# A fused cross-attention, block and router loop on one Trainium2 core: PSUM banks by stage, three choice batches, spread first weights, and block one-hots multiplied on GpSimd

## The chip, the cores and the metric

The kernel runs on one core of one Trainium2 chip. The metric is the device time of one execution in microseconds, the median over runs. The engines are named as in the profile: PE (TensorE, with PEld for its weight loads), DVE (VectorE), ACT (ScalarE), POOL (GpSimd) and SP (SyncE, which here only issues DMAs). They run their own instruction streams and meet at semaphores.

## The reference

Shapes: x is 8 sequences of 512 tokens, 512 wide; the context is 8 sequences of 77 rows. Cut to what matters:

```
x = x + cross_attention(layernorm(x), ctx)     # 16 heads of 32, softmax over 77 keys, wo, bo
h  = attention block on groups of 8 tokens      # (512 positions are the batch): LN1, qkv (4 kv heads), causal
h1 = x + proj(h)
z2 = LN2(h1);  logits = z2 @ router_weight      # 8 experts
top 2 of 8 by softmax, renormalised             # share = p1 / (p1 + p2), which needs only exp(l2 - l1)
order = stable sort of (token, choice) by expert; first `cap` rows of each expert are kept
out = h1 + scatter_add(share * gelu(xt @ w1[e]) @ w2[e])
```

## The kernel before, in words

The 4096 tokens are 32 tiles of 128. One Python loop of 52 steps (`STEPS`) writes, for every engine, what it does in step i; it is a software pipeline, in which a tile is in another stage in each step. Tile t = i − 1 is transposed (`xT`, kind `xt`), i − 2 gets its scores (and q, for two tiles at once, in even steps), i − 4 has its probabilities transposed (`pT`, four jobs of kind `pt`) and multiplied with the values (`pv`), i − 5 goes through `wo`. From step 13 the same loop also carries block tiles f, with lags from `FF` = 14: the first layer norm (statistics `mvf`, normalised tile z, kept in `ctx_then_block`) at lag FF − 1, its transposes and qkv, scores, projection, second layer norm, router logits, and at lag FF + 5 the softmax over the two best experts. So steps 3 to 13 are cross attention only, 14 to 18 fill the block's pipeline, 19 to 33 carry both, and from 36 only the block is left. The loop is followed by the choice of experts, the search for each row's slot, one-hot matrices from which PE makes the table of rows (`one_hots`), and then the experts.

What the prediction's steps touch:

- PSUM has eight banks. `psum_plan` hands them out in the order of `psum_jobs`, in turn within each half; a score job `s` takes banks 0 to 3 together. `bank_free` makes PE wait until the old user of a bank is read out.
- First layer norm of f: DVE takes the statistics (L668, L669); POOL adds and takes a power −0.5 (L508, L509, giving `rff` for z and the semaphore `rstd_f`), and then another pair with another constant (L437, L438, giving `rf` for the residual); DVE makes z (L907). After this POOL multiplies the probabilities by the softmax's reciprocals (L448).
- Router softmax of f: DVE takes the eight largest (L865) and the `gap` of the first two (L867); ACT takes `ex` = exp(gap) (L620); POOL makes the shares in five operations (L494 to L501), which stand on POOL ahead of L508.
- DVE turns q and k of the block in L879 and L883; L883 waits for `v_kept`, a copy on ACT (L615).
- Choice: `choose(a, b)` on DVE makes the 0/1 matrix `both` of tiles a to b − 1 in 10 operations (L692 to L699), at the end of a step; `count_places` on PE counts with three matmuls per tile (L934 to L938), one step later. `CHOICES` says in which step which tiles go.
- The first expert's weights come in eight pieces of 128 x 1024, one in each of the steps 39 to 46: SP loads one, ACT rounds the high part, POOL subtracts for the low part (L1155), behind everything else of its step.
- `one_hots`: eight batches of eight tiles. ACT makes the row one-hots of six tiles (`BY_ACT`; L652, L657), DVE those of the other two (L748), the block one-hots `is_blk` (L744) and their product with token numbers `hot_blk` (L751); PE multiplies the two (L1071).

## Time and profile before

| | |
|---|---|
| median of 3 runs | 1679.21 us (1679.16 to 1680.63) |
| the profiled execution's own time | 1678.78 us |
| its span, first to last instruction | 1677.0 us |
| mean granted TensorE clock | 0.959 of full speed |
| PE busy | 1520.7 us, 91% of the span |
| DVE, POOL, ACT busy | 951.9, 837.0, 713.4 us |

Times in the trace count from the start of the span. In it step 3 begins at about 45 us, step 14 at 205, step 19 at 317, step 34 at 650, step 39 at 726, step 47 at 837; the search for slots begins at about 880 and the experts at 905. An idle time in brackets stands before the instruction that it delayed, with the instruction that released it.

### The profile page before, as it was taken

The numbers are of one execution on the slowest core, as the hardware profiler recorded it, in microseconds if no ns is written. First come the engines' busy times: TensorE is split into PE (matmuls) and PEld (weight loads), VectorE is DVE, ScalarE is ACT, GpSimd is POOL, SyncE is SP. The second block draws the span as 40 slices with busy tenths as digits, with TensorE's granted clock in tenths as the row PEclk, the third lists the DMA queues.
The fourth block names the chain that finished last, engine by engine and source line by source line (L and its number), as shares of the span: only waits on it lengthen the run. The fifth ranks groups of instructions, "written<-read, shape, count | busy, mean of one in ns | idle before, by whom it ended". The sixth has DMA issues, their size and how long they took to land. (4 is left out here: it accounts for less than half of the span.)

```text
span 1677.0 us, 30921 instructions
## 1 busy us (share of the span) xinstructions
PE 1520.7 (91%) x11103; PEld 1325.8 (79%) x11104; DVE 951.9 (57%) x1780; ACT 713.4 (43%) x1448; POOL 837.0 (50%) x953
## 2 busy tenths in 40 slices
PE   7788788999999999998863999899999979999986
PEld 5566677888888888877752989899999869899975
DVE  4766656777777767677756445543233555343361
ACT  2343443555554455455435434433332534343341
POOL 1343444556655556678741637453343665463242
PEclk9999889999999999999975999999999989999999
DMA  6111211122222212222211424343442533442221
GB/s 240 39 51 58 70 51 51 46 76 77 71 67 67 66 63 72 69 95 79 80 57 55 102 57 105 75 110 68 90 89 41 110 98 76 97 102 51 36 40 23
DMA packets 63597, 124.58 MB, mean 74 GB/s; under 512 B 13232, under 2 KB 13648, under 8 KB 62921
## 3 DMA queue, kind: packets, MB, share of 16 engines
q1 hardware_dynamic: 45184, 92.54, 16.9%
q0 software_dynamic: 17920, 29.31, 10.4%
q8 instruction: 108, 1.77, 0.5%
q10 hardware_dynamic: 328, 0.50, 0.1%
q14 instruction: 57, 0.46, 0.1%
HBM read 89.02 MB, written 46.27 MB: 81 GB/s over the span
## 5 line engine op out<-in xcount | busy, mean ns | idle before, releaser
L1351 PEld LDWEIGHTS hidden_ps<-gT,w 128*128 128x128 f32 x2880 | 350.4, 192 | 9.1 <-ACT hT L1270 4.2
L1351 PE MATMUL hidden_ps<-gT,w 128*128 128x256 f32 x2880 | 352.7, 284 | 5.3 <-ACT hT L1270 3.2
L1380 PE MATMUL expert_ps<-w,hT 128*128 128x512 f32 x1440 | 341.7, 397 | 8.1 <-DVE og L1320 8.1
L1380 PEld LDWEIGHTS expert_ps<-w,hT 128*128 128x128 f32 x1440 | 272.4, 191 | 65.9 <-DVE og L1320 8.5
L1295 DVE TENSOR_TENSOR hT<-gl,hT 128x512 fp32r<-128x512 f32 x160 | 130.5, 824 | 250.4 <-ACT hT L1270 250.3
L1155 POOL TENSOR_TENSOR w<-raw,w 128x1024 fp32r<-128x1024 f32 x64 | 155.0, 2433 | 201.2 <-ACT w L1149 200.8
L1268 ACT ACTIVATE gl<-hidden_ps 128x512 f32<-128x512 f32 x160 | 95.7, 598 | 335.3 <-PE hidden_ps L1351 312.6
L1252 POOL DMA_INDIRECT out_dram<-og,idx x80 | 130.3, 1628 | 153.7 <-DVE og L1320 140.0
L1320 DVE TENSOR_SCALAR og<-expert_ps,kept 128x512 f32<-128x512 f32 x80 | 59.1, 749 | 159.0 <-PE expert_ps L1380 154.9
L1278 ACT ACTIVATE gT<-yk 128x256 fp32r<-128x256 f32 x160 | 66.9, 418 | 109.1 <-DVE yk L1306 107.3
L1024 PE MATMUL main_ps<-wqkv_hi,zT 128*128 128x512 f32 x256 | 109.0, 441 | 4.8 <-DVE h L798 4.8
L1242 POOL DMA_INDIRECT xg<-normed_tokens,idx x80 | 86.4, 1080 | 48.9 <-POOL idx L1237 33.6
L811 DVE TENSOR_TENSOR x<-main_ps,xc 128x512 f32<-128x512 f32 x32 | 22.1, 692 | 153.7 <-PE main_ps L342 153.7
L961 PE MATMUL main_ps<-small,pr 128*77 128x128 f32 x512 | 74.5, 290 | 33.8 <-DVE xT_lo L788 15.6
L606 ACT ACTIVATE pr<-pr 128x616 f32<-128x616 f32 x64 | 45.6, 718 | 132.1 <-DVE pr L846 132.1
L1270 ACT ACTIVATE hT<-hidden_ps 128x512 fp32r<-128x512 f32 x160 | 95.3, 596 | 14.8 <-PE expert_ps L1380 14.8
L961 PEld LDWEIGHTS main_ps<-small,pr 128*77 128x77 f32 x512 | 61.9, 157 | 42.4 <-issue 26.6
L448 POOL TENSOR_TENSOR pr<-pr,rec 128x616 f32<-128x616 f32 x64 | 76.7, 1218 | 31.2 <-DVE rec L901 31.2
L1306 DVE TENSOR_SCALAR yk<-gather_ps,small 128x256 f32<-128x256 f32 x160 | 83.1, 540 | 2.9
L488 POOL TENSOR_TENSOR ctx_then_block<-ctx_then_block,rec 128x512 f32<-128x512 f32 x32 | 33.8, 1057 | 93.9 <-DVE rec L861 93.8
L342 PE MATMUL main_ps<-xT_hi,wq_hi 128*128 128x256 f32 x256 | 75.7, 296 | 4.0 <-DVE xT_lo L788 4.0
L556 ACT ACTIVATE pT<-main_ps 77x512 f32<-77x512 f32 x128 | 69.1, 592 | 22.9 <-PE main_ps L961 21.0
(178 smaller groups left out, 3225.6 us busy)
## 6 DMA issues: line engine op xcount, KB each, us to landing
raw<-L_ffn_moe_w_dram SPq DMA_DIRECT2D x64, 512.0 KB, 3.6
normed_tokens<-h SPq DMA_DIRECT2D x128, 65.0 KB
xa<-x_dram SPq DMA_DIRECT2D x32, 256.0 KB, 2.7
xc<-x_dram SPq DMA_DIRECT2D x32, 256.0 KB, 3.0
attended_rows<-x SPq DMA_DIRECT2D x32, 256.0 KB, 2.0
fx<-attended_rows SPq DMA_DIRECT2D x128, 64.0 KB
out_dram<-fx SPq DMA_DIRECT2D x128, 64.0 KB
fx<-qkv_rows_dram SPq DMA_DIRECT2D x1, 1536.0 KB, 6.6
```

What stands on the lines that cost most here:

```text
L448: pool.tensor_tensor(shares, shares, bc(rec[:, t % 2, 8 * half:8 * half + 8], 2, [P, 8, SK]), ALU.mult).then_inc(s["shared"], 1)
L961: last = pe.transpose(bank("pt", tp, b)[0:SK, g * P:(g + 1) * P], pr[:, tp % 2, b, g, :], ident)
L1024: last = pe.matmul(bank("qkv", fq, 0), zT[fq % 2][l][:, k, :], wqkv[r][:, k, 0:D], start=k == 0 and n == 0, stop=k == KT - 1 and n == 2)
L1155: pool.tensor_tensor(weight_piece(p, 1, j), raw[:, j % 2, :], weight_piece(p, 0, j).bitcast(F32), ALU.subtract).then_inc(s["w_lo"], 1)
L1242: pool.indirect_dma_start(out=xg[:, g.s % 2, k, :], out_offset=None, in_=z2d[:, :], in_offset=rows(g, k), bounds_check=N - 1, oob_is_err=F ...
L1252: pool.indirect_dma_start(out=out2d[:, :], out_offset=rows(g, k), in_=og[:, k, :], in_offset=None, bounds_check=N - 1, oob_is_err=False, c ...
L1268: act.activation(gl[:, q % 2, :], pH[:, q, :], ACT.Gelu_apprx_tanh)
L1270: act.activation(hT[g.s % 2][0][:, 2 * q:2 * q + 2, :].rearrange("p f n -> p (f n)"), pH[:, q, :], ACT.Gelu_apprx_tanh).then_inc(s["gelu"], 1)
L1295: dve.tensor_tensor(o[1], gl[:, q % 2, :], o[0].bitcast(F32), ALU.subtract)\
L1306: dve.tensor_scalar(yk[:, k % 2, :].rearrange("p (b n) -> p b n", b=GB), pT[:, :, k * P:(k + 1) * P], ln2w[:, k:k + 1], ln2b[:, k:k + 1], ...
L1351: last = pe.matmul(pH[:, q, f * W:(f + 1) * W], w1[p][l][:, k, cols], xT[g.s % 2][r][:, k, :], start=k == 0 and n == 0, stop=k == KT - 1 a ...
L1380: last = pe.matmul(pY[:, k, :], hT[par][l][:, f, k * P:(k + 1) * P], w2[p][r][:, f, :], start=f == 0 and n == 0, stop=f == FT - 1 and n == 2)
```

## The change

1. In steps below 14, `psum_plan` puts each kind of job into banks of its own (`OWN_BANKS`). Where a job takes bank 0 or 1 from a score job, `bank_free` now waits only for the first half of the scores to be read.
2. Six choice batches become three: tiles 0 to 27 in step 48, 28 to 30 in step 50, 31 behind the loop. `choose` now stands near the start of DVE's step, no longer at its end.
3. The eight pieces of the first weights are loaded in steps 38, 40, 42, 44, 46, 47, 48, 49 and split one step later (before: loaded in 38 to 45).
4. GpSimd multiplies the block one-hots by the token numbers; ACT makes the row one-hots of four tiles rather than six, DVE those of the other four.
5. POOL's two powers of the first layer norm become one over two columns (`rf` is now 8 x 2); z waits for that one.
6. DVE's L865 and L867 (largest eight, gap) move from ahead of the turn of q to behind the turn of k, so ahead of the statistics of the next tile.
7. In the start, ACT rounds `wq` ahead of four DMA issues, and a block of step 1 moves to step 2.

```diff
-BY_ACT = 6
+BY_ACT = 4
+OWN_BANKS = {"pt": 0, "q": 0, "xt": 4, "wo": 5, "val": 6, "pv": 7}
-CHOICES = ((LATE, 0, 9), (LATE + 2, 9, 18), (LATE + 6, 18, 24), (LATE + 10, 24, 28), (STEPS - 2, 28, 31),
-           (STEPS, 31, 32))
+FIRST_PIECES = {LATE: (0,), LATE + 2: (1,), LATE + 4: (2,), LATE + 6: (3,), LATE + 8: (4,), LATE + 9: (5,),
+                LATE + 10: (6,), LATE + 11: (7,)}
+CHOICES = ((STEPS - 4, 0, 28), (STEPS - 2, 28, 31), (STEPS, 31, 32))
...
-            if kind == "s":
+            if i < FF and kind in OWN_BANKS:
+                take((kind, t, j), [OWN_BANKS[kind] + j])
+            elif kind == "s":
...
-                pe.wait_ge(*read_out[old](t_old, j_old))
+                if old == "s" and kind != "s" and place[kind, t, j] < 2:
+                    pe.wait_ge(s["shifted"], 2 * t_old + 1)
+                else:
+                    pe.wait_ge(*read_out[old](t_old, j_old))
...
-                    link(pool, "pool_link", linked,
-                         pool.tensor_scalar(wf[:, 0:1], var, 1.0 + EPS, EPS * EPS, ALU.mult, ALU.add))
-                    pool.tensor_tensor(rff[:, f % 2:f % 2 + 1], wf[:, 0:1], expo[:, 0:1], ALU.pow)\
-                        .then_inc(s["rstd_f"], 1)
+                    pool.tensor_scalar(wf[:, 0:1], var, 1.0 + EPS, EPS * EPS, ALU.mult, ALU.add)
+                    link(pool, "pool_link", linked, pool.tensor_scalar(wf[:, 1:2], var, EPS, None, ALU.add))
                     need(pool, s["h0_done"], f - 7)
-                    link(pool, "pool_link", linked, power(rf[:, f % 8:f % 8 + 1], var, wf[:, 1:2]))
+                    pool.tensor_tensor(rf[:, f % 8, :], wf[:, :], expo[:, :], ALU.pow).then_inc(s["rstd_f"], 1)
+                    pool.wait_ge(s["rstd_f"], f + 1)
...
+            for b in range(2 * NT // BATCH):
...
+                pool.wait_ge(s["blks"], b + 1)
+                need(pool, s["tabled"], b - 1)
+                pool.tensor_tensor(choice["hot_blk"][:, b % 2, :, :], choice["is_blk"][:, b % 2, :, :],
+                                   bc(number[:, tiles], 2, [P, BATCH, NBLK]), ALU.mult).then_inc(s["hots"], 1)
...
+            act.wait_ge(wq_in, 16)
+            act.activation(wq[0][:, :, :], rq, ACT.Copy).then_inc(s["wq_hi"], 1)
             act.dma_start(x2[0:TB, 0, 0:P], a["token_sel"]).then_inc(tok_in, 16)
...
-            act.wait_ge(wq_in, 16)
-            act.activation(wq[0][:, :, :], rq, ACT.Copy).then_inc(s["wq_hi"], 1)
...
-                if i == 1:
+                if i == 2:
...
                 if i == 0 or i > EARLY_LOW:
                     low_halves(i)
+                batch = chosen(i, 0)
+                if batch is not None:
+                    choose(*batch)
...
-                f = tile(i, FF + 5)
-                if f is not None:
-                    dve.wait_ge(s["lg_evac"], f + 1)
-                    chained(dve.max(tops[:, f, :], logits[:, f, :]))
-                    need(dve, s["gap_exp"], f)
-                    dve.tensor_tensor(gap[:, :], tops[:, f, 1:2], tops[:, f, 0:1], ALU.subtract).then_inc(s["gap"], 1)
...
                     k_turn.then_inc(s["k_turned"], 1)
+                f = tile(i, FF + 5)
+                if f is not None:
+                    dve.wait_ge(s["lg_evac"], f + 1)
+                    chained(dve.max(tops[:, f, :], logits[:, f, :]))
+                    need(dve, s["gap_exp"], f)
+                    dve.tensor_tensor(gap[:, :], tops[:, f, 1:2], tops[:, f, 0:1], ALU.subtract).then_inc(s["gap"], 1)
...
-                batch = chosen(i, 0)
-                if batch is not None:
-                    choose(*batch)
```

On DVE, the end of a step that carries both attentions (a piece of the order before; in square brackets the semaphores that an instruction waits for):

```order
L860 TENSOR_REDUCE exp_sums2<-ctx_then_block 128x16 [waits shared2,exp2]
L861 RECIPROCAL rec2<-exp_sums2 128x16 [waits dve_link]
L865 MAX tops<-logits 128x8 [waits lg_evac]
L867 TENSOR_TENSOR gap<-tops 128x1 [waits gap_exp,dve_link]
L879 STREAM_TRANSPOSE ctx_then_block<-main_ps 128x512 [waits s2_mm,cleared,qkv_mm]
L883 STREAM_TRANSPOSE ctx_then_block<-main_ps 32x4x32 [waits v_kept]
L883 STREAM_TRANSPOSE ctx_then_block<-main_ps 32x4x32 x3
L668 BN_STATS bnf<-fx 128x6 [waits shift_f,fx_in4]
```

The same place of the changed kernel, with its own line numbers:

```order
L878 TENSOR_REDUCE exp_sums2<-ctx_then_block 128x16 [waits shared2,exp2]
L879 RECIPROCAL rec2<-exp_sums2 128x16 [waits dve_link]
L891 STREAM_TRANSPOSE ctx_then_block<-main_ps 128x512 [waits s2_mm,cleared,qkv_mm]
L895 STREAM_TRANSPOSE ctx_then_block<-main_ps 32x4x32 [waits v_kept]
L895 STREAM_TRANSPOSE ctx_then_block<-main_ps 32x4x32 x3
L901 MAX tops<-logits 128x8 [waits lg_evac]
L903 TENSOR_TENSOR gap<-tops 128x1 [waits gap_exp,dve_link]
L684 BN_STATS bnf<-fx 128x6 [waits shift_f,fx_in4]
```

The pair that starts the router softmax now stands behind the turns of q and k and their wait for `v_kept`.

On POOL, the end of the same step, before:

```order
L488 TENSOR_TENSOR ctx_then_block<-ctx_then_block,rec2 128x512 [waits rec2_done]
L494 TENSOR_SCALAR share_sum<-ex 128x1 [waits gap_exp]
L496 TENSOR_TENSOR share<-share_sum,expo2 128x1 [waits pool_link]
L497 TENSOR_TENSOR share<-ex,share 128x1 [waits pool_link]
L499 TENSOR_SCALAR same<-logits,tops,share 128x8
L501 TENSOR_SCALAR h1<-same,share 128x8 [waits pool_link]
L508 TENSOR_SCALAR wf<-mvf 128x1 [waits stat_f]
L509 TENSOR_TENSOR rff<-wf,expo 128x1 [waits pool_link]
L437 TENSOR_SCALAR wf<-mvf 128x1 [waits h0_done]
L438 TENSOR_TENSOR rf<-wf,expo 128x1 [waits pool_link]
L513 TENSOR_SCALAR shift<-mvf,rf 128x1 [waits pool_link]
L448 TENSOR_TENSOR pr<-pr,rec 128x616 [waits rec_done] x2
```

And in the changed kernel:

```order
L495 TENSOR_TENSOR ctx_then_block<-ctx_then_block,rec2 128x512 [waits rec2_done]
L501 TENSOR_SCALAR share_sum<-ex 128x1 [waits gap_exp]
L503 TENSOR_TENSOR share<-share_sum,expo2 128x1 [waits pool_link]
L504 TENSOR_TENSOR share<-ex,share 128x1 [waits pool_link]
L506 TENSOR_SCALAR same<-logits,tops,share 128x8
L508 TENSOR_SCALAR h1<-same,share 128x8 [waits pool_link]
L514 TENSOR_SCALAR wf<-mvf 128x1 [waits stat_f]
L515 TENSOR_SCALAR wf<-mvf 128x1
L517 TENSOR_TENSOR rf<-wf,expo 128x2 [waits h0_done,pool_link]
L519 TENSOR_SCALAR shift<-mvf,rf 128x1 [waits rstd_f]
L455 TENSOR_TENSOR pr<-pr,rec 128x616 [waits rec_done] x2
```

Ahead of the power that z waits for there is one more small instruction than before, behind it a pair less; all stand behind the shares of the router softmax, as before.

## Rows read from the trace of the kernel before

**Rows 1.** Busy time in stretches (us; instructions in brackets; granted clock, DMA share, GB/s).

```profile
317.00:650.00 333.00, 326.28 (x2847) 282.50 (x2848) 246.92 (x485) 173.89 (x384) 199.07 (x308) 1.00 0.21 69
837.00:880.00 43.00, 27.98 (x157) 23.21 (x155) 22.98 (x72) 13.18 (x35) 20.09 (x38) 0.77 0.15 55
```

**Rows 2.** PE's waits from 300 to 720 us: total us, times, longest.

```profile
PE main_ps L1053 <- DVE ctx_then_block L879: 3.7, 15, 0.3
PE main_ps L961 <- DVE xT_lo L788: 3.3, 14, 0.8
```

**Rows 3.** Timeline of an odd step with both attentions (start us, us, instruction).

```profile
556.57 0.72 DVE L879 STREAM_TRANSPOSE ctx_then_block<-main_ps 128x512 f32<-128x512 f32 x1
557.21 1.25 DVE L883 STREAM_TRANSPOSE ctx_then_block<-main_ps 32x128 f32<-32x128 f32 x4
557.62 0.22 POOL L494 TENSOR_SCALAR share_sum<-ex 128x1 f32<-128x1 f32 x1
559.65 0.19 POOL L508 TENSOR_SCALAR wf<-mvf 128x1 f32<-128x1 f32 x1
559.93 0.57 POOL L509 TENSOR_TENSOR rff<-wf,expo 128x1 f32<-128x1 f32 x1
561.14 0.54 DVE L907 TENSOR_SCALAR ctx_then_block<-fx,mvf,rff 128x512 f32<-128x512 f32 x1
562.61 0.69 DVE L788 TENSOR_TENSOR xT_lo<-main_ps,xT_hi 128x512 fp32r<-128x512 f32 x1 [0.20 <-ACT xT_hi L543]
```

**Rows 4.** Timeline of step 38, block only, from one z to the next.

```profile
713.10 0.55 DVE L907 TENSOR_SCALAR ctx_then_block<-fx,mvf,rff 128x512 f32<-128x512 f32 x1 [1.06 <-POOL rff L509]
722.25 1.29 DVE L883 STREAM_TRANSPOSE ctx_then_block<-main_ps 32x128 f32<-32x128 f32 x4
725.55 0.55 DVE L907 TENSOR_SCALAR ctx_then_block<-fx,mvf,rff 128x512 f32<-128x512 f32 x1 [1.06 <-POOL rff L509]
```

**Rows 5.** Timeline: gap of step 50 and POOL's answer to it.

```profile
873.69 0.16 DVE L867 TENSOR_TENSOR gap<-tops 128x1 f32<-128x1 f32 x1
...
874.17 0.22 POOL L494 TENSOR_SCALAR share_sum<-ex 128x1 f32<-128x1 f32 x1 [3.01 <-ACT ex L620]
```

**Rows 6.** Timeline of a step between 14 and 18.

```profile
244.74 0.54 DVE L907 TENSOR_SCALAR ctx_then_block<-fx,mvf,rff 128x512 f32<-128x512 f32 x1
245.37 2.38 POOL L448 TENSOR_TENSOR pr<-pr,rec 128x616 f32<-128x616 f32 x2
246.74 1.11 PE L961 MATMUL main_ps<-small,pr 128*77 128x128 f32 x4 [3.42 <-DVE xT_lo L788]
```

**Rows 7.** Timeline of steps 38 and 44: DVE beside POOL.

```profile
718.72 1.53 POOL L476 TENSOR_TENSOR vbd<-ctx_then_block,small 128x512 f32<-128x512 f32 x1
...
719.25 1.28 DVE L854 TENSOR_SCALAR h<-h,mvh,rh 128x512 f32<-128x512 f32 x1
...
814.95 2.36 POOL L1155 TENSOR_TENSOR w<-raw,w 128x1024 fp32r<-128x1024 f32 x1
815.08 2.30 DVE L692 TENSOR_TENSOR equal<-rest,tops 128x48 f32<-128x48 f32 x1
```

**Rows 8.** Timeline of an even step of cross attention only (step 12).

```profile
178.89 1.23 PE L961 MATMUL main_ps<-small,pr 128*77 128x128 f32 x8 [2.72 <-DVE oT_lo L782]
```

**Rows 9.** Timeline of PE: counting six tiles (first, last), and four at 869 us.

```profile
830.00 0.28 PE L934 MATMUL main_ps<-both,orders 128*128 128x256 f16 x1
...
831.03 0.17 PE L938 MATMUL main_ps<-both,orders 128*128 128x8 f16 x1
...
869.55 0.42 PE L934 MATMUL main_ps<-both,orders 128*128 128x256 f16 x1
...
870.68 0.17 PE L938 MATMUL main_ps<-both,orders 128*128 128x8 f16 x1
```

**Rows 10.** Instructions by line from 880 to 904 us (busy us, mean ns | idle before).

```profile
L652 ACT ACTIVATE distance<-ramp,row 128x128 f16<-128x128 f16 x48 | 14.8, 386 | 6.5 <-DVE row L729 6.5
L751 DVE TENSOR_TENSOR hot_blk<-is_blk,consts 128x640 f16<-128x640 f16 x8 | 6.6, 820 | 0.0
```

More of the change, by code:

```diff
@@ L237, in build_main @@
     token_mask = sb("token_mask", [TB, 16 * TB], F32R)
-    expo = sb("expo", [P, 1])
+    expo = sb("expo", [P, 2])
     fx = sb("fx", [P, FX, D])
@@ L275, in build_main @@
     wx, wf, wh = sb("wx", [P, 1]), sb("wf", [P, 2]), sb("wh", [P, 1])
-    rx, rf, rff, rh = sb("rx", [P, 2]), sb("rf", [P, 8]), sb("rff", [P, 2]), sb("rh", [P, 2])
+    rx, rf, rh = sb("rx", [P, 2]), sb("rf", [P, 8, 2]), sb("rh", [P, 2])
     shift = sb("shift", [P, 8])
@@ L301, in build_main @@
                  "lg_mm lg_evac cleared dve_link pool_link "
-                 "consts_done counted gap gap_exp weighed prefixed found blks act_rows hots tabled xg_cleared dist").split()
+                 "consts_done counted gap gap_exp weighed prefixed found blks act_rows hots tabled xg_cleared dist dve_rows").split()
         s = {n: sem(n) for n in names}
@@ L423, in _ @@
                     sp.dma_start(choice["product"][:, 0:3 * P], a["routing_orders"]).then_inc(const_in, 16)
-                if 0 <= i - LATE < CH:
+                for j in FIRST_PIECES.get(i, ()):
                     sp.wait_ge(s["x2_done"], NT)
-                    weights["load"](sp, 0, 0, 0, i - LATE)
+                    weights["load"](sp, 0, 0, 0, j)
             for f in range(NT - FX, NT):
@@ L525, in _ @@
                     pool.memset(groups["xg"][:, :, :, :], 0.0).then_inc(s["xg_cleared"], 1)
-                if 0 <= i - LATE - 1 < CH:
-                    weights["low"](pool, 0, 0, i - LATE - 1)
+                for j in FIRST_PIECES.get(i - 1, ()):
+                    weights["low"](pool, 0, 0, j)
             pool.wait_ge(s["xg_cleared"], 1)
+            start, n = CONST_PLACES["number"]
+            number = choice["consts"][:, start:start + n]
+            pool.wait_ge(const_in, 32)
+            for b in range(2 * NT // BATCH):
+                part_no = b % (NT // BATCH)
+                tiles = slice(part_no * BATCH, (part_no + 1) * BATCH)
+                pool.wait_ge(s["blks"], b + 1)
+                need(pool, s["tabled"], b - 1)
+                pool.tensor_tensor(choice["hot_blk"][:, b % 2, :, :], choice["is_blk"][:, b % 2, :, :],
+                                   bc(number[:, tiles], 2, [P, BATCH, NBLK]), ALU.mult).then_inc(s["hots"], 1)
         @block.scalar
         def _(act):
+            act.wait_ge(wq_in, 16)
+            act.activation(wq[0][:, :, :], rq, ACT.Copy).then_inc(s["wq_hi"], 1)
             act.dma_start(x2[0:TB, 0, 0:P], a["token_sel"]).then_inc(tok_in, 16)
@@ L590, in _ @@
                     act.activation(h1[:, f % 4, 0:D], fx[:, f % FX, :], ACT.Identity, bias=shift[:, f % 8:f % 8 + 1],
-                                   scale=rf[:, f % 8:f % 8 + 1]).then_inc(s["h0_done"], 1)
+                                   scale=rf[:, f % 8, 1:2]).then_inc(s["h0_done"], 1)
                 f = tile(i, FF + 2)
@@ L642, in _ @@
                         .then_inc(s["consts_done"], 1)
-                if 0 <= i - LATE - 1 < CH:
-                    weights["high"](act, 0, 0, i - LATE - 1)
+                for j in FIRST_PIECES.get(i - 1, ()):
+                    weights["high"](act, 0, 0, j)
             act.wait_ge(s["found"], 1)
@@ L741, in one_hots @@
                     shape = [P, BATCH, NBLK]
-                    is_blk, hot_blk = choice["is_blk"][:, b % 2, :, :], choice["hot_blk"][:, b % 2, :, :]
+                    is_blk = choice["is_blk"][:, b % 2, :, :]
                     need(dve, s["hots"], b - 1)
@@ L748, in one_hots @@
                     dve.tensor_tensor(choice["hot_row"][:, b % 2, BY_ACT:BATCH, :], bc(ramp, 1, shape_rows),
-                                      bc(row[:, k, rest_tiles], 2, shape_rows), ALU.is_equal)
-                    dve.wait_ge(s["blks"], b + 1)
-                    dve.tensor_tensor(hot_blk, is_blk, bc(number[:, tiles], 2, shape), ALU.mult).then_inc(s["hots"], 1)
+                                      bc(row[:, k, rest_tiles], 2, shape_rows), ALU.is_equal)\
+                       .then_inc(s["dve_rows"], 1)
             def write_rows():
@@ L906, in _ @@
                     need(dve, s["zt_mm"], f)
-                    dve.tensor_scalar(z, fx[:, f % FX, :], mvf[:, f % 2, 0:1], rff[:, f % 2:f % 2 + 1],
+                    dve.tensor_scalar(z, fx[:, f % FX, :], mvf[:, f % 2, 0:1], rf[:, f % 8, 0:1],
                                       ALU.subtract, ALU.mult).then_inc(s["z_done"], 1)
-                batch = chosen(i, 0)
-                if batch is not None:
-                    choose(*batch)
             last_tile(CHOICES[-1][1])
@@ L1069, in _ @@
                 pe.wait_ge(s["act_rows"], b + 1)
+                pe.wait_ge(s["dve_rows"], b + 1)
                 for n in range(BATCH):
@@ L1083, in routing_buffers @@
                "is_blk": sb("is_blk", [P, 2, BATCH, NBLK], F16), "hot_blk": sb("hot_blk", [P, 2, BATCH, NBLK], F16),
-               "equal": sb("equal", [P, 9, E]), "hot": sb("hot", [P, 2, NT, E]), "rest": sb("rest", [P, NT, E]),
+               "equal": sb("equal", [P, NT, E]), "hot": sb("hot", [P, 2, NT, E]), "rest": sb("rest", [P, NT, E]),
                "product": sb("product", [P, 2 * NT * E]), "empty": sb("empty", [P, NBLK]),
```

2 lines of the change are left out of this document (1 added, 1 removed).

## The prediction

> **What bounds the kernel now.** I read the busy time by stretches first. While both attentions run, PE is busy 326.3 of 333.0 us at full clock [rows 1]; only some 7 us can be won there, but a new stall on PE's path is paid in full. From step 36 on, only the block is left and each tile waits for the one before: a latency chain, in which a delay counts even where no engine is full. Between 837 and 880 us PE is busy 28.0 of 43.0 us at a granted clock of 0.77 [rows 1]. The experts behind 905 us are untouched.
>
> Then PE's waits. From 300 to 720 us two are left: for the turn of q (3.7 us in 15 waits) and for `xT_lo` (3.3 us in 14) [rows 2]. The timeline shows what stands ahead of `xT_lo`: z at 561.14, then `oT_lo`, then `xT_lo`, idle for only 0.20 us before it and done at 563.30 [rows 3]. z needs POOL's power, which ends at 560.50: it is 0.64 us early [rows 3]. In the block-only steps nothing is early: z itself waits 1.06 us for that power, and one z follows the other by 12.45 us [rows 4]. So a change to what POOL does ahead of the power is read at z.
>
> **Gap behind the turns, one power instead of two.** All sums are against the profiled execution's 1678.78 us; the median lies 0.43 us above it.
>
> *Steps 19 to 31, 13 of them.* The turn of q starts 0.26 us earlier, the time that L865 and L867 took. The turn of k waits for `v_kept` (there at 557.06 in that timeline) and so gains only 0.11: 557.10 to 558.35. DVE's instructions overlap by some 0.08, so L865 starts at 558.27, L867 0.15 later at 558.42. From the start of a gap to POOL's first share operation are 874.17 − 873.69 = 0.48 us [rows 5]: POOL begins the shares at 558.90 where it began at 557.62, 1.28 later. From there to the first add (L508) are 2.03 us [rows 3]: 560.93. Then the first add (0.19), the second (0.28, as from L508 to L509), the power (0.57, and 0.05 taken for its second column; bounds nothing, and 0.57 if columns went one by one): 562.02. z starts at about 562.04, 0.90 late. `oT_lo` follows by 0.58, `xT_lo` by 0.61 and takes 0.69: it ends at 563.92 instead of 563.30. PE, which was waiting for it already, loses **0.62 us** per step, 8.1 in all. The 0.25 us per step that PE gains at the turn of q [rows 2] lie ahead of the same wait and vanish in it. In steps 32 to 34 no x is left, and that gain stays: −0.7.
>
> *Steps 14 to 18.* There is no gap yet. Here POOL's order matters: the old second pair of adds and power delayed L448 to 245.37, behind z's start at 244.74; its input was there at 243.92. With one power POOL is free about 0.9 us sooner and the probabilities' product of 2 x 1.19 us [rows 6] starts about 244.45, ahead of z. While POOL runs a long product, DVE is held up: L854, a subtract-and-multiply of z's form, takes 1.28 us beside POOL's L476 (0.53 elsewhere), and the choice's L692 2.30 instead of 0.20 beside POOL's L1155 of 2.36, which began 0.13 us earlier [rows 7]. z is then done with the first half of L448, about 245.65, instead of 245.28, and with the order of the three that follow (`oT_lo`, `xT_lo` held by the second half) I take 0.7 us at `xT_lo`, for which PE waits there (3.42 us, ended by it) [rows 6]. 5 × 0.7 = 3.5; bounds nothing (L448 starts behind z as before) and 1.2 a step (a whole half).
>
> *Steps 35 and 36*: z late by 1.7 us each as the two cases meet, 3.4.
>
> *Steps 37 to 44.* The turn of k starts 9.12 us after the z before it [rows 4]; with 1.29 us for it, less 0.08, plus 0.15, the gap starts at +10.48, the shares at +10.96, the first add at +12.99, the power's end at +14.08: **14.1 us** from z to z where it was 12.45. With a weight piece ahead of it (three of the eight steps) I take 14.5, by the 0.4 us that such a piece still holds DVE. Eight steps are 5 × 14.1 + 3 × 14.5 = 114.0. Before, the eight took 112.7 (from z at 700.65 to z at 813.40, rows like [rows 4]); of these 13.1 were above 8 × 12.45, for choices, counts and pieces. Most of that is gone, and the later gap gives it back: +1.3.
>
> **The choice.** *Step 45* loses a choice of 4.5 us (2.30 of it the lock of [rows 7]), a count of 1.07 us and the PE time at a low clock behind them: from z at 813.40 to the block's next transposes at 831.06 were 17.7 us, and 12.2 remain: −5.5. *Step 48* gains ten operations of 128 x 224. Operations of 72, 48 and 24 elements take 0.23, 0.21 and 0.18 us, so 224 take about 0.40 by their slope, and ten some 4.3 with their hops. DVE idles 4.06 us at that place (to 854.10), but POOL's L488, the shares and a piece of 2.4 us run in it, and hold up those choice operations that POOL catches: the next LN2 starts 2.8 late (0 if all fits, 3.6 if all is in series). *The count* of 28 tiles stands between two dependent matmul groups of the last tile. Six tiles took 1.20 us at full clock, four took 1.30 at 869 us [rows 9]; 28 take 5.6 or 9.1, 10 with the longer ones for early tiles. I take 7.3, between the two since the count itself keeps PE busy; against the 1.3 of four tiles and some idle time, the last logits come 4.5 late (2.7 to 8.2). *Step 50* has its choice no longer behind the gap (−2.1), but the last weight piece runs into the search for slots (+0.9): −1.2.
>
> **One-hots.** A batch takes 2.72 us now, from the six row one-hots of one batch on ACT to the next: six times 0.386, with overlap 1.84 [rows 10], and the 0.93 of L657. With four ACT has 1.87. DVE has 0.82 for `is_blk` (as much as L751 [rows 10]) and 0.69 for four tiles' row one-hots; POOL multiplies 640 elements: by L448, 616 in 1.19, that is 1.23 (bounds 1.2, and 1.5 by L1155's 1024 in 2.36). If DVE and POOL hold each other up as in [rows 7], the three follow each other: 0.82 + 0.69 + 1.23 = 2.74, less two seams of 0.13: 2.48 a batch, −1.5 with the ends of the loop. Without contention ACT would bound it at 1.87: −6.9. With slow multiplies and no seam: +1.3. I take the middle, since [rows 7] shows the hold-up in this kernel.
>
> The Trainium skill (SBUF — State Buffer, "Who interferes with whom") says that a DVE instruction with two SBUF inputs and a GpSimd instruction that reads SBUF use one shared port pair, that whoever issues first holds it for the whole instruction, and that the other blocks fully. By that rule there is no seam, a batch is 2.74 us and the one-hots are no faster than before (+0.2), 1.7 us more than my term. The hold-up of 2.30 beside 2.36 us agrees in kind; the 0.13 us overlap of the two rows speaks for my value.
>
> **PSUM banks and the start.** The waits that the banks should shorten are large: 2.72 us for `oT_lo` in an even step [rows 8]. But q follows in the same step and needs `xT_lo`, which in that timeline ends at 179.34, about 0.45 after PE is released now; an earlier `pt` only moves the idle time. Even steps gain 0.44 each (four) and 0.65 (step 4), step 11 0.35, step 13 1.5 (z of x no longer behind POOL's L484), the start 0.5: −4.5, between −1 (all absorbed) and −7. The weights' new times cost nothing by themselves: their loads end long before the experts, since the search for slots lies between.
>
> **Sum.** −4.5 + 3.5 + 8.1 − 0.7 + 3.4 + 1.3 − 5.5 + 2.8 + 4.5 − 1.2 − 1.5 = +10.2; **1689.0 us**. Runs can tell about 0.2% (3.4 us) from no change.
>
> **Rivals.**
> *The later gap costs nothing* (faster). POOL's power had 0.64 us to spare in the fused steps; Shares that come up to 0.64 later, less the second add, cost nothing, and 0.20 more of z's delay goes into DVE's idle time. If `v_kept` and `ex` come 0.3 us sooner than I worked out, 8.1 shrinks to about 4; if POOL gets the adds in before the shares, all delay goes: 8.1, 3.5 and 3.4 become 0, and steps 37 to 44 take 8 × 12.45 and 0.4 for each of three pieces, 100.8 against 112.7: −11.9 instead of +1.3, together 1660.8. All stalls that I price come to 8.1 + 3.5 + 3.4 + 13.2 = 28.2 us; this case decides the sign where they are under 64% of that. For it: only tenths separate the cases. Against it: the order on POOL is fixed, the shares ahead of the adds.
> *The clock falls.* Steps 36 on leave PE 1.6 us more idle in each period, and between 837 and 880 us, where it idles most, the granted clock is 0.77 [rows 1]. If it does so from step 38, matmuls of about 5 us a period at half speed cost 1.5 us each in part of the periods: +10, 1700.
> *The tail is hidden*: GpSimd's product costs no contention (−5.4), the choice of step 48 fits into DVE's idle time (−2.8): 1681, no change.
> *The banks do nothing*, as q waits for x: +3.5, 1693, inside the range.
>
> **How the numbers follow.** My forecast, with the banks' rival, 0.55; falling clock 0.12; hidden tail 0.15; no cost of the later gap 0.18. Faster: 0.18 and a little of the tail's case, 0.20. Same: 0.15 of the tail's case and the forecast's low edge, 0.15. Slower: 0.65. The low end goes to 1676, two thirds into the gap between forecast and first rival; the high end to 1701. For the forecast alone: 1683 to 1696.
>
> **What would show it.** In the fused steps: POOL's shares start about 1.3 us later in the step and z waits for `rstd_f`; PE's waits for `xT_lo` grow from 3.3 to about 11 us. From step 37: 14.1 us between z's. At 850 us: ten choice operations of 0.4 us, some of 2. The count: 28 tiles in 6 to 9 us. One-hots: 2.5 us between PE's groups. I am wrong if z's start does not move against the turn of k, or if the period from step 37 falls below 12.5 us.

## The result

The changed kernel takes 1713.76 us (median of 4 runs, 1710.38 to 1715.39) where before takes 1679.92: a ratio of 1.0198 (95% interval 1.0179 to 1.0217), 34 us slower. The sign was as forecast; the size is three times the +10.2 us that I summed, and the time lies 12.8 us above the top of the range. One of the four executions of the kernel with both parts back (below) took 1917 us at a mean granted clock of 0.737, and its ratio leaves that one out.

The spans of the two profiled executions (1713.2 and 1677.0 us) differ by 36.2 us. I cut both at the same instructions: the starts of the first z of the loop, of those of steps 19, 32, 36 and 44, and of the first `is_blk`.

| stretch | before | changed | difference | my terms |
|---|---|---|---|---|
| start to first z (step 13) | 208.9 | 204.4 | −4.5 | −4.5 |
| to z of step 19 | 126.1 | 133.7 | +7.6 | +4.1 |
| to z of step 32 | 296.9 | 310.7 | +13.8 | +8.1 |
| to z of step 36 | 68.8 | 71.8 | +3.0 | +2.1 |
| to z of step 44 | 112.8 | 126.4 | +13.7 | +1.3 |
| to the first `is_blk` | 67.7 | 72.4 | +4.7 | +0.6 |
| one-hots | 23.2 | 21.1 | −2.1 | −1.5 |
| experts | 772.7 | 772.7 | 0.0 | 0 |

(The terms go into the stretches as nearly as their places allow. The z of step 19 is itself late by one step's loss, so 0.6 stands in the second row and is missing in the fourth.) The start and the first eleven steps differ by up to 4.7 us between executions of one order (in five kernels without the bank plan the first z came between 206.9 and 211.6 us), so the first row alone shows little.

**The profile after.** PE's waits from 300 to 740 us answer to [rows 2]; `xT_lo` is now waited for 21.9 us in the same 14 waits:

```profile
PE main_ps L976 <- DVE xT_lo L803: 21.9, 14, 1.7
PE main_ps L937 <- DVE ctx_then_block L925: 6.8, 3, 2.7
```

The timeline of an odd step with both attentions (a fused step, below), which answers to [rows 3] (POOL's L495, the old L488, starts 12.33 us later than there, and so all times):

```profile
569.43 1.29 DVE L895 STREAM_TRANSPOSE ctx_then_block<-main_ps 32x128 f32<-32x128 f32 x4
570.75 0.17 DVE L901 MAX8 tops<-logits 128x8 f32<-128x8 f32 x1
570.96 0.16 DVE L903 TENSOR_TENSOR gap<-tops 128x1 f32<-128x1 f32 x1
...
571.44 0.22 POOL L501 TENSOR_SCALAR share_sum<-ex 128x1 f32<-128x1 f32 x1 [1.58 <-ACT ex L636]
...
573.51 0.19 POOL L514 TENSOR_SCALAR wf<-mvf 128x1 f32<-128x1 f32 x1
...
573.76 0.23 POOL L515 TENSOR_SCALAR wf<-mvf 128x1 f32<-128x1 f32 x1
...
574.08 0.73 POOL L517 TENSOR_TENSOR rf<-wf,expo 128x2 f32<-128x2 f32 x1
...
574.84 0.55 DVE L925 TENSOR_SCALAR ctx_then_block<-fx,mvf,rf 128x512 f32<-128x512 f32 x1 [1.06 <-POOL rf L517]
...
576.85 0.63 PE L976 MATMUL main_ps<-small,pr 128*77 128x128 f32 x4 [1.58 <-DVE xT_lo L803]
```

The reader can follow the chain from one bracket to the next: POOL idles 1.58 us for `ex`, z waits 1.06 us for POOL, PE waits 1.58 us for what stands behind z. That is the mechanism that I had forecast. Taken back by 12.33 us, the shares start at 559.11 (I had 558.90) and z at 562.51 (I had 562.04).

The steps with the block only answer to [rows 4]. Timeline of two z and what follows them on PE:

```profile
752.53 0.55 DVE L925 TENSOR_SCALAR ctx_then_block<-fx,mvf,rf 128x512 f32<-128x512 f32 x1 [2.88 <-POOL rf L517]
...
753.13 0.66 PE L937 MATMUL main_ps<-small,ctx_then_block 128*128 128x128 f32 x4 [2.63 <-DVE ctx_then_block L925]
...
754.14 1.52 PE L1007 MATMUL main_ps<-ctx_then_block 128*128 128x128 f32 x8
```

```profile
768.70 0.55 DVE L925 TENSOR_SCALAR ctx_then_block<-fx,mvf,rf 128x512 f32<-128x512 f32 x1 [2.89 <-POOL rf L517]
...
770.31 1.16 PE L1007 MATMUL main_ps<-ctx_then_block 128*128 128x128 f32 x8
```

z waits 2.9 us for POOL instead of 1.06, and PE 2.6 us for z. The same eight matmuls then take 1.52 us in one step and 1.16 in the next. The windows from z to z say why (length, busy PE, PEld, DVE, ACT, POOL, with instructions in brackets; then the granted clock, DMA share, GB/s):

```profile
737.98:752.53 14.55, 11.92 (x73) 10.13 (x73) 9.81 (x20) 7.25 (x18) 9.20 (x15) 1.00 0.27 92
752.53:768.70 16.17, 13.49 (x73) 11.60 (x73) 9.68 (x20) 7.59 (x17) 10.49 (x16) 0.89 0.14 49
768.70:783.57 14.87, 12.13 (x73) 10.12 (x73) 10.39 (x20) 6.75 (x16) 11.53 (x16) 1.00 0.30 89
```

At full clock a period is 14.55 us, 14.87 with a weight piece; where the granted clock is 0.89 as a mean (part of the period at 1.2 GHz instead of 2.4) the same instructions take 16.2, and in step 37, at 0.80, 17.5. Five of the eight are such periods. In the one of 16.17 all of the 1.6 us lie ahead of the turn of k, which starts 10.76 us behind z instead of 9.16: the chain goes through PE's matmuls up to there, and from there to the next z it takes as long as at full clock.

### The profile page after: what moved, and what is told of

It is laid out like the page before. It is cut to its first block and busy times, and to the rows that moved or that the text cites. A ratio compares the mean times of both kernels' runs of the same rounds, so it can differ in the third digit from the quotient of the medians.

```text
span 1713.2 us, 30874 instructions
## 1 busy us (share of the span) xinstructions
PE 1528.6 (89%) x11103; PEld 1335.2 (78%) x11104; DVE 954.4 (56%) x1742; ACT 705.4 (41%) x1432; POOL 835.6 (49%) x929
## 3 DMA queue, kind: packets, MB, share of 16 engines
q0 software_dynamic: 17920, 29.31, 10.2%
## 5 line engine op out<-in xcount | busy, mean ns | idle before, releaser
L495 POOL TENSOR_TENSOR ctx_then_block<-ctx_then_block,rec 128x512 f32<-128x512 f32 x32 | 33.6, 1050 | 98.0 <-DVE rec L879 98.0
```

## The experiments

Each kernel is compared with before on the same chip. The first four undo or reorder parts of the changed kernel.

**The gap back ahead of the turn of q.**

```diff
+                f = tile(i, FF + 5)
+                if f is not None:
+                    dve.wait_ge(s["lg_evac"], f + 1)
+                    chained(dve.max(tops[:, f, :], logits[:, f, :]))
+                    need(dve, s["gap_exp"], f)
+                    dve.tensor_tensor(gap[:, :], tops[:, f, 1:2], tops[:, f, 0:1], ALU.subtract).then_inc(s["gap"], 1)
                 t = tile(i, 2)
                 if t is not None and t < S:
                     dve.wait_ge(s["val_mm"], t + 1)
...
                     k_turn.then_inc(s["k_turned"], 1)
-                f = tile(i, FF + 5)
-                if f is not None:
-                    dve.wait_ge(s["lg_evac"], f + 1)
...
```

> The changed kernel with one part undone: DVE takes the largest eight and the gap ahead of the turn of q again; all else stays. Theory (the late gap makes POOL's shares, and behind them the power and z, late): the period of the fused steps falls from 22.6+1.06 back to that of before, the block-only period from 14.6 to about 12.6, and the whole falls by 13 x 1.06 + 8 x 2 + the clock's loss, to some 1680 us or below. Rival 1 (the merged power is the cost: 0.73 us instead of 0.57 and a second add ahead of it): about a third of the loss goes, some 1703 us, and z still waits for POOL by more than 1.06 us. Rival 2 (banks, choice or pieces cost it): no change, 1714 us.

1672.16 us, ratio 0.9958 (0.9942 to 0.9975): this one placement is worth 41.6 us. From the z of step 19 to that of step 32 it takes 296.8 us (before 296.9), from step 36 to 44 105.5 us, steps 37 to 44 all at clock 1.00. The theory stands; the merged power as the only cause falls.

**Two powers again, gap late.**

```diff
-                    pool.tensor_scalar(wf[:, 0:1], var, 1.0 + EPS, EPS * EPS, ALU.mult, ALU.add)
-                    link(pool, "pool_link", linked, pool.tensor_scalar(wf[:, 1:2], var, EPS, None, ALU.add))
+                    link(pool, "pool_link", linked,
+                         pool.tensor_scalar(wf[:, 0:1], var, 1.0 + EPS, EPS * EPS, ALU.mult, ALU.add))
+                    pool.tensor_tensor(rf[:, f % 8, 0:1], wf[:, 0:1], expo[:, 0:1], ALU.pow).then_inc(s["rstd_f"], 1)
                     need(pool, s["h0_done"], f - 7)
-                    pool.tensor_tensor(rf[:, f % 8, :], wf[:, :], expo[:, :], ALU.pow).then_inc(s["rstd_f"], 1)
-                    pool.wait_ge(s["rstd_f"], f + 1)
+                    link(pool, "pool_link", linked, power(rf[:, f % 8, 1:2], var, wf[:, 1:2]))
```

> The changed kernel with one part undone: POOL takes two powers of one column again, the one for z first; the gap stays late. Theory (late gap): z comes only about 0.4 us sooner (one add of 0.25, 0.16 of the power): 13 x 0.4 + 8 x 0.4, and 3 to 4 us in steps 14 to 18 where the probabilities' product falls behind z again: about 1701 us. Rival 1 (the merged power is the cost): 1685 us or below. Rival 2: 1714 us.

1707.4 us, ratio 1.0158 (1.0140 to 1.0176): 6.4 us come back, half of what I expected, and not by the parts that I gave. The fused steps lose 0.72 us each instead of 1.06. From step 36 on, though POOL is done sooner, all eight periods are longer than most of the changed kernel's, 17.1 to 17.2 us, at clock 0.80. Here the size of the loss in these steps (137.2 us against 126.4 and 112.8) follows the clock and not POOL.

**Both back.** The two edits above together; in short:

```diff
+                f = tile(i, FF + 5)
+                if f is not None:
+                    dve.wait_ge(s["lg_evac"], f + 1)
...
-                    pool.tensor_tensor(rf[:, f % 8, :], wf[:, :], expo[:, :], ALU.pow).then_inc(s["rstd_f"], 1)
+                    link(pool, "pool_link", linked, power(rf[:, f % 8, 1:2], var, wf[:, 1:2]))
```

> The changed kernel with both parts undone (early gap and two powers); banks, choice, pieces, block one-hots on GpSimd and the start stay as changed. By my terms these leave -4.5 (banks and start), a period of 12.45 and no choice in steps 37 to 44 (-11), -5.5 in step 45, +2.8 and +4.5 in the tail, -1.5 in the one-hots: about 1665 us. Rival (the new choice and count cost more than they give, or the clock): 1680 us or above.

1663.73 us, ratio 0.9904 (0.9885 to 0.9924). What is left of the change is a gain of 1%, as my terms for banks, choice and one-hots gave. Steps 36 to 44 take 102.7 us (before 112.8).

**The first norm ahead of the shares on POOL.** Gap late, power merged; the two blocks on POOL change places.

```diff
+                f = tile(i, FF - 1)
+                if f is not None:
+                    pool.wait_ge(s["stat_f"], f + 1)
...
                 f = tile(i, FF + 5)
                 if f is not None:
                     pool.wait_ge(s["gap_exp"], f + 1)
...
-                f = tile(i, FF - 1)
-                if f is not None:
-                    pool.wait_ge(s["stat_f"], f + 1)
...
```

> The changed kernel with its late gap and its merged power, but POOL does the first layer norm's adds and power ahead of the router's shares. Theory (z is late because the power stands behind shares that wait for the late gap): z no longer waits, the fused steps lose their 1.06 us and the block-only period falls to about 13 us: 1680 us or below although the gap is as late as before. Rival (the late gap costs through DVE or ACT themselves): 1710 us.

1680.04 us, ratio 0.9995 (0.9983 to 1.0006). With the gap as late as in the changed kernel, 33.7 us are gone, and the period of step 38 is 13.08 us at clock 1.00. So most of the late gap's cost comes from POOL's order: the power stands behind shares that wait for the gap. Not all of it: 7.9 us more than with the early gap (1672.16) are left, 3.7 of them in steps 19 to 31 of the profiles (300.5 against 296.8 us).

The next ones put one part alone into the kernel before.

**Banks alone** (`OWN_BANKS` and the wait for half the scores).

```diff
+OWN_BANKS = {"pt": 0, "q": 0, "xt": 4, "wo": 5, "val": 6, "pv": 7}
...
+            if i < FF and kind in OWN_BANKS:
+                take((kind, t, j), [OWN_BANKS[kind] + j])
...
```

> The kernel before with only the PSUM banks by stage and the wait for half the scores. My term for it was about -4 (-0.5 to -6.5): 1676 us. With both the early gap and the two powers back, the first z came 7.3 us earlier than before; if the banks make that, it is -7 here (1673 us), if the start makes part of it, less. Rival (q waits for its x anyway): 1680 us.

1673.07 us, ratio 0.9950 (0.9934 to 0.9967). The waits of PE from 45 to 205 us change hands more than they shrink. Before, its largest were

```profile
PE main_ps L961 <- DVE oT_lo L782: 12.0, 9, 2.7
```

and with the banks

```profile
PE main_ps L967 <- DVE pr L852: 10.3, 7, 3.1
```

The first z comes at 203.4 us as a mean of the nine profiled kernels that have the banks (201.2 to 205.8; eight of them have the changed start too), and at 208.9 in the five that don't: 5.5 us. In this kernel's own profile it comes at 205.4. The timed gain is 5.5 to 11 us by its interval. So the rival falls, and 7 us from the banks alone, as the expectation had it, is possible; how much the start gives was not tried by itself.

**The late gap alone.**

```diff
-                f = tile(i, FF + 5)
-                if f is not None:
-                    dve.wait_ge(s["lg_evac"], f + 1)
...
                     k_turn.then_inc(s["k_turned"], 1)
+                f = tile(i, FF + 5)
+                if f is not None:
+                    dve.wait_ge(s["lg_evac"], f + 1)
...
```

> The kernel before with only the gap moved behind the turn of k. Theory: in the fused steps z waits for POOL, +0.6 to +0.9 a step (9.5 us in 13 steps); from step 37 on the period goes to about 14 us at full clock and to 17 us where PE's clock falls, on top of the old choices: 1679.9 + 9.5 + 15 to 35, so 1705 to 1725 us. Rival (the move costs only beside the other edits): below 1690 us.

1706.73 us, ratio 1.0156 (1.0139 to 1.0173). The 13 steps from 19 on lose 9.3 us, 0.72 each; steps 36 to 44 take 128.5 us, 15.8 more than before, five of their eight periods below full clock.

**One power alone** (the merged power in the kernel before, gap early).

```diff
...
-                    pool.tensor_tensor(rff[:, f % 2:f % 2 + 1], wf[:, 0:1], expo[:, 0:1], ALU.pow)\
-                        .then_inc(s["rstd_f"], 1)
...
-                    link(pool, "pool_link", linked, power(rf[:, f % 8:f % 8 + 1], var, wf[:, 1:2]))
...
+                    pool.tensor_tensor(rf[:, f % 8, :], wf[:, :], expo[:, :], ALU.pow).then_inc(s["rstd_f"], 1)
+                    pool.wait_ge(s["rstd_f"], f + 1)
```

> The kernel before with only the merged power of the first norm. Theory: in steps 14 to 19 the product of the probabilities on POOL now starts ahead of z and holds it up, 0.6 to 0.9 us a step (4 us, as my term of 3.5 said); in the fused steps nothing; from step 37 on z waits 0.47 us longer for the wider power, in 6 of 8 steps and less where a choice covers it; together 6 to 8 us: 1686 us. Rival (the merged power costs only beside the late gap): 1680 us.

1687.46 us, ratio 1.0052 (1.0036 to 1.0068). From the first z to step 19 it loses 3.5 us, in steps 19 to 32 nothing, from 36 to 44 1.0. These rows are of an execution of 1684.01 us; what the median has above it is not placed. The timeline of step 15:

```profile
246.27 2.57 POOL L448 TENSOR_TENSOR pr<-pr,rec 128x616 f32<-128x616 f32 x2
246.31 1.45 DVE L906 TENSOR_SCALAR ctx_then_block<-fx,mvf,rf 128x512 f32<-128x512 f32 x1
...
249.23 1.10 PE L960 MATMUL main_ps<-small,pr 128*77 128x128 f32 x4 [4.33 <-DVE xT_lo L787]
```

Against [rows 6]: POOL's product starts 0.04 us ahead of z instead of 0.63 behind it, z takes 1.45 us instead of 0.54, and PE waits 4.33 us instead of 3.42. In every profiled kernel with the merged power z takes 1.44 to 1.46 us in steps 14 to 18, and 0.55 in every one with two.

**The choice alone** (three batches, at the start of DVE's step).

```diff
-CHOICES = ((LATE, 0, 9), (LATE + 2, 9, 18), (LATE + 6, 18, 24), (LATE + 10, 24, 28), (STEPS - 2, 28, 31),
-           (STEPS, 31, 32))
+CHOICES = ((STEPS - 4, 0, 28), (STEPS - 2, 28, 31), (STEPS, 31, 32))
...
```

> The kernel before with only the three choice batches at the start of DVE's step. My terms: steps 37 to 44 from 112.7 to about 104 (-8.6), step 45 -5.5, the choice in step 48 +2.8 and the count of 28 tiles +4.5, the choice of step 50 -2: about -9, 1671 us. Rival (the tail gives all back): 1680 us.

1671.1 us, ratio 0.9942 (0.9924 to 0.9960). Steps 36 to 44 take 104.0 us, as expected, and from there to the first `is_blk` 66.1 instead of 67.7.

**One-hots alone.**

```diff
-BY_ACT = 6
+BY_ACT = 4
...
+                pool.tensor_tensor(choice["hot_blk"][:, b % 2, :, :], choice["is_blk"][:, b % 2, :, :],
+                                   bc(number[:, tiles], 2, [P, BATCH, NBLK]), ALU.mult).then_inc(s["hots"], 1)
...
```

> The kernel before with only the block one-hots multiplied on GpSimd and four tiles' row one-hots on each of ACT and DVE. From the changed kernel's rows: 2.40 us a batch instead of 2.72, the stage from 23.2 to 21.1 us: -2.1, 1677.5 us. Rival (without the hold-up 1.9 a batch): -6.5.

1677.78 us, ratio 0.9996 (0.9985 to 1.0007): the runs can't tell it from no change. Its profiled execution shows the stretch from the first `is_blk` to the end of the table at 21.1 us instead of 23.2, as in the changed kernel. The lines of the changed kernel that answer to [rows 10]:

```profile
L760 DVE TENSOR_TENSOR is_blk<-ramp,blk 128x640 f16<-128x640 f16 x8 | 13.9, 1742 | 0.0
L543 POOL TENSOR_TENSOR hot_blk<-is_blk,consts 128x640 f16<-128x640 f16 x8 | 13.0, 1624 | 7.6 <-DVE is_blk L760 7.6
```

`is_blk` takes 1.74 us as a mean, where L751 of the same size took 0.82: it waits inside for POOL. A batch takes 2.40 us (from one `is_blk` to the next, 923.05 to 925.45). The first batch of the changed kernel and the third, on DVE and POOL:

```profile
920.05 0.69 DVE L764 TENSOR_TENSOR hot_row<-ramp,row 128x512 f16<-128x512 f16 x1
...
920.30 1.54 POOL L543 TENSOR_TENSOR hot_blk<-is_blk,consts 128x640 f16<-128x640 f16 x1 [2.30 <-DVE is_blk L760]
920.65 1.88 DVE L760 TENSOR_TENSOR is_blk<-ramp,blk 128x640 f16<-128x640 f16 x1
...
924.85 0.68 DVE L764 TENSOR_TENSOR hot_row<-ramp,row 128x512 f16<-128x512 f16 x1
925.00 1.64 POOL L543 TENSOR_TENSOR hot_blk<-is_blk,consts 128x640 f16<-128x640 f16 x1 [0.76 <-DVE is_blk L760]
925.45 1.87 DVE L760 TENSOR_TENSOR is_blk<-ramp,blk 128x640 f16<-128x640 f16 x1
```

In all eight batches the multiply ends 1.11 or 1.12 us behind the row one-hots, whether it began 0.43 us ahead of their end (the first) or 0.52, and the next `is_blk` ends 0.68 us behind the multiply. So the three follow each other in turn.

The last three test the clock and follow the findings.

**Busy PE.** The kernel with two powers and the late gap, with eight matmuls that nothing reads ahead of PE's wait for z in steps 39 to 44.

```diff
                 if fz is not None:
+                    if i > LATE:
+                        for old, t_old, j_old in ousted["table", 0, 0]:
+                            pe.wait_ge(*read_out[old](t_old, j_old))
+                        for n in range(8):
+                            pe.matmul(ps[:, place["table", 0, 0], :], wpj[0][:, n % KT, 0:P], wpj[0][:, n % KT, :],
+                                      start=True, stop=True)
                     pe.wait_ge(s["z_done"], fz + 1)
```

> The changed kernel with two powers (1707.4 us, 17.1 us a period from step 37 on at a granted clock of 0.80), in which PE does eight matmuls more of 128 x 512, into a bank that is free, while it waits for z in steps 39 to 44; nothing reads them. If the idle time makes the clock fall and the clock makes 17.1 of 14.1, these periods fall to 14 to 14.5 us at clock 1.00 although PE has more to do: about 1707 - 6 x 2.8 = 1690 us. Rival (the 17.1 us are latency of the engines' chain, the clock only follows): still 17.1 a period or more, 1707 us.

1689.56 us: 17.8 us less than without these matmuls (by the ratios to before, 1.0054 and 1.0158, 17.5). Two windows from z to z of the kernel without them:

```profile
776.49:793.62 17.13, 14.93 (x73) 12.64 (x73) 9.30 (x20) 7.58 (x17) 9.15 (x16) 0.80 0.13 47
793.62:810.71 17.09, 14.91 (x73) 12.60 (x73) 9.88 (x20) 6.75 (x16) 11.45 (x17) 0.80 0.24 78
```

and with them:

```profile
772.44:786.53 14.09, 14.09 (x84) 11.71 (x82) 9.81 (x20) 7.58 (x17) 9.65 (x16) 1.00 0.18 58
786.53:800.91 14.38, 13.59 (x81) 11.33 (x80) 10.36 (x21) 6.75 (x16) 12.12 (x17) 1.00 0.27 93
```

PE has more to do and each period is 2.7 to 3.0 us shorter. So 14.1 us (14.4 with a weight piece) is the chain's own latency here, and the rest is the clock, which was low because PE idled in that wait. That I had worked out 14.1 too is chance: mine was for the merged power, whose chain takes 14.55.

**Count early.** Both parts back, and PE counts a batch ahead of its wait for the last tile's second norm.

```diff
+                batch = chosen(i, 1)
+                if batch is not None:
+                    count_places(*batch)
                 if ft is not None:
                     pe.wait_ge(s["z2_done"], ft + 1)
...
-                batch = chosen(i, 1)
-                if batch is not None:
-                    count_places(*batch)
```

> Early gap and two powers (1663.7 us), and PE counts a batch ahead of its wait for the last tile's second norm instead of behind the transposes of that. PE idled 3.86 us there and the 28 tiles took 7.2 us at first low, then full clock. Theory (the count is on the path of the last tile, the idle time ahead of it is free): 3 to 4 us of it vanish and the clock is up sooner: 1659 to 1660 us. Rival (the last tile's logits wait for ACT anyway): 1663.7 us.

1662.46 us, ratio 0.9899 (0.9881 to 0.9917), not to be told from 0.9904. In the profile the last two tiles' largest-eight come 5.5 us apart instead of 9.6, but the search for slots then starts 1.4 us later behind them, since POOL's last weight piece now meets it: of the 4.1 us 2.7 are left at the first `is_blk`.

**Count and statistics early.** In addition, from step 37 on, the first norm's statistics stand where DVE idles, and its powers ahead of the shares.

```diff
+                f = tile(i, FF - 1)
+                if f is not None and i >= LATE - 1:      # ahead of a_lo
+                    dve.wait_ge(fx_in[f % FX], 64 * (f // FX + 1))
+                    need(dve, s["shift_f"], f - 1)
+                    stats(fx[:, f % FX, :], bnf, mvf[:, f % 2, :]).then_inc(s["stat_f"], 1)
                 f = tile(i, FF + 3)
                 if f is not None:
                     dve.wait_ge(s["a_hi"], f + 1)
```

> The kernel of the run before it, and from step 37 on DVE takes the first norm's statistics ahead of the low half of the attention output, where it idles, and POOL does that norm's adds and powers ahead of the router's shares. Theory (from step 37 on the chain of z through POOL sets the period): z no longer waits, the period falls from 12.45 and 13.1 to PE's own 12.1: 7 x 0.35 and 4 x 0.65 = 5 us less than count_early, 1655 us. Rival (PE's own 12.1 us with its small waits are the bound already, or the pieces of POOL just collide elsewhere): no more than 1.5 us less.

1659.37 us, ratio 0.9872 (0.9852 to 0.9893), the fastest here and some 20 us below before. Its periods after the first are 12.1 to 12.8 us instead of 12.45 to 13.55, with PE busy 11.9 of them. The 3.1 us below the kernel ahead of it are between the two expectations, and the intervals overlap.

## Why the prediction was wrong

Point by point, by the terms of the sum. In the two profiles the sum is 26.0 us short: 12.4 in steps 37 to 44, which is the step that failed, 5.7 in steps 19 to 31, 4.1 behind step 44, 3.5 from the first z to step 19, and 0.3 in the other rows.

- *Steps 19 to 31, +0.62 each; measured 1.06.* The mechanism is right, as the timeline, the undone gap and the swapped order on POOL show. The size failed in "DVE's instructions overlap by some 0.08" and in the power. L901 starts 0.03 us behind the end of the turn of k and the gap 0.21 behind L901, not 0.15: the shares come 0.21 us later than I had. The hop, the two adds and the wider power took another 0.26 (the power 0.73 where I took 0.62 and had allowed up to 1.14). With one power alone nothing is lost in these steps, with the late gap alone 0.72, with both 1.06: the slack of 0.64 us that z had hides the wider power where it is the only delay, and behind the late gap it is paid.
- *Steps 32 to 36, −0.7 and +3.4:* the fourth row shows +3.0 for my 2.1.
- *Steps 14 to 18, +3.5; measured 3.5 for the merged power alone.* z is held up as forecast, by 0.9 us; but `oT_lo` and `xT_lo` take 0.69 each as before and are not held by the product's second half, so that part of the 0.7 a step was wrong and its size partly luck. In the changed kernel the stretch lost 7.6: 1.4 are a late gap in step 19, and about 1.5 are step 17, where the granted clock was 0.85 and in before 0.92. The remaining 1.2 lie in the first period, which took 19.0 us here and 17.5 to 20.2 in other kernels, also with the early gap: they say nothing of the change.
- *Steps 37 to 44, +1.3; measured +13.7.* This is the step that failed. The chain's latency was 14.55 us (14.87 with a piece) where I had 14.1 (14.5), by the same 0.2 for the gap and 0.26 behind it: at full clock the eight periods would be some 117.4 us, 3.4 more than I said. The other 9.0 us are the clock. I had this as a rival with 0.12 and a price of 10, set apart from the forecast, when the forecast itself leads to it: z later by 1.7 us means PE idle by 1.7 us more in each period, and no row spoke for a clock that would bear this. But one row of before did speak against it. In the first of the two periods in which a choice held z up the granted clock was 0.90 (in the other, of 16.99 us, 1.00):

```profile
725.55:740.50 14.95, 12.57 (x69) 10.13 (x68) 12.51 (x31) 7.69 (x17) 11.38 (x17) 0.90 0.28 88
```

  With 9.0 for the clock and 3.4 for the latency the sum would have been 1701, still 12 us too low by the other terms.
- *Step 45, −5.5*, and the choice of step 48, +2.8. From the z of step 44 to the block's gap two tiles on was 24.6 us before, 25.4 in the changed kernel, but 19.8 with the choice alone: the gain of −4.7 is real, and with the late gap it is gone: I had priced it with the early gap's period. The choice in step 48 cost 2.5, one of its operations 2.01 instead of 0.39 us beside a weight piece; with the choice alone, where no piece lies in that step, it cost 0.85.
- *The count, +4.5; measured +4.8.* The 28 tiles took 7.46 us (I had 7.3), at first with 0.38 us a matmul, later with 0.27, as the clock rises under them. PE's rows, which answer to [rows 9]:

```profile
903.35 1.12 PE L937 MATMUL main_ps<-small,h 128*128 128x128 f32 x4 [3.86 <-DVE h L872]
904.26 0.42 PE L949 MATMUL main_ps<-both,orders 128*128 128x256 f16 x1
...
911.56 0.27 PE L949 MATMUL main_ps<-both,orders 128*128 128x256 f16 x1
911.72 1.04 PE L1044 MATMUL main_ps<-small,ctx_then_block 128*128 128x8 f32 x8
```

- *Step 50, −1.2; measured −1.3,* from the last tile's largest eight to the first `is_blk` (7.59 us before, 6.30 changed).
- *One-hots, −1.5; measured −2.1.* They hold each other up as forecast: 2.40 a batch against 2.48. The three follow each other, and the 1.62 us of POOL's multiply hold its wait for the row one-hots, as the 1.87 of `is_blk` hold one for the multiply. By the ends of the rows above the multiply alone takes about 1.12 (an estimate), where I had 1.23: 0.83 + 0.68 + 1.12 = 2.63, less seams of 0.23 together, where I had 0.26. The Trainium skill (SBUF — State Buffer, "Who interferes with whom") has the shared port pair as an exclusive lock; the trace agrees in that the three run in turn, and not in that there would be no seam.
- *Banks and start, −4.5; measured −5.5* as the difference of the means of the first z, −4.5 in the pair of profiles above, with a spread between executions nearly as large as the term.

The rival on the other side (the later gap costs nothing) was wrong for the order on POOL that the change has. With the order swapped most of the cost goes, as that rival had it, but the 1680.04 us stay 19 above its 1661.

The parts alone add up to +16 us (−8.4 banks, −9.7 choice, −0.7 one-hots, +8.7 power, +26.2 gap, by their ratios); together they are +33. The new steps of the weight pieces and the changed start were not tried alone. In the profiles most of what the parts lack lies in three stretches: 4.6 us in steps 19 to 31, where the wider power is hidden alone and paid behind the late gap; 6.8 in steps 37 to 44; and 7.9 from there to the first `is_blk`, 2.9 of them where the choice's gain lay and 3.4 in step 48, where a choice operation now meets a weight piece at its new time. For steps 37 to 44 the rows of the late gap alone show one reason:

```profile
728.17:745.37 17.20, 15.01 (x73) 12.67 (x73) 9.31 (x21) 7.24 (x18) 9.14 (x16) 0.80 0.23 77
745.37:762.57 17.20, 16.60 (x97) 14.27 (x98) 12.60 (x30) 7.09 (x16) 11.37 (x17) 0.80 0.24 77
762.57:776.93 14.36, 12.65 (x79) 10.42 (x77) 10.36 (x20) 8.18 (x18) 12.12 (x17) 1.00 0.27 92
```

In the second of these periods PE counts the first nine tiles just ahead of z, in the time in which it idled 2.2 us in the period before, and the next period is at full clock. The changed kernel has no counts in these steps, and two powers again, which has none either, stays at 0.80 over all eight (137.2 us, against 128.5 with the old choices). So the choices that went away had also kept PE busy where it now waits. That this makes up the 6.8 us is not shown. What stays open is why the merged power, which is the longer, leaves three of the changed kernel's eight periods at full clock, and two powers leave none. It may differ between executions: two of the four of two powers again were 5 us shorter, at a mean granted clock of 0.950 and 0.949 where the profiled one had 0.944.

## What to carry to other kernels

Before an instruction is moved behind a wait, list what stands behind its consumer on the consumer's engine, in program order: here two instructions of 0.26 us on DVE held a power on POOL that had nothing to do with them. In a stretch that is a latency chain, price a delay twice: once as latency, and once as TensorE's idle time, since a lower granted clock made 17.1 us of 14.1; here some matmuls that nobody reads brought it back, and so did a count that stood in that wait. Gains that were worked out for the old period have to be worked out again for the new one; and work that is taken out of a wait can have kept the clock up.

## What the runs showed of the hardware that was not expected

- The granted clock fell in a stretch where PE was still busy 12 us of every 14.5, with one wait of 2.2 to 2.7 us in each period. Once low, it stayed low over eight periods in one kernel (0.80 throughout) and went up and down in another.
- A power of two columns on GpSimd took 0.73 us where one of one column took 0.57.
- A DVE subtract-and-multiply of 128x512 that starts 0.04 us behind a GpSimd product took 1.45 us instead of 0.54: it ended 0.28 us behind the first half of that product, which ran from 246.27 to 247.48.
- A GpSimd multiply of 128x640 that starts 0.43 or 0.52 us ahead of the end of a DVE compare of 128x512 ended 1.11 to 1.12 us behind that end in all eight batches: its 1.54 or 1.64 us hold the wait.
